# Attention on 64x64 array tiles in two shared PSUM banks, windows at a pitch of 64, no value masks, new order of all engines: a windowed-attention image kernel on one Trainium2 core

## What is computed

```python
def _swin_block(x, shift, mask, ...):
    sc = x
    x = _ln(x, ln1g, ln1b)
    if shift: x = jnp.roll(x, (-shift, -shift), axis=(1, 2))
    qkv = _win_part(x) @ qkvw + qkvb
    q, k, v = heads of 32 ...
    attn = jnp.einsum('whid,whjd->whij', q, k) * HEAD_DIM ** (-0.5)
    attn = softmax(attn + bias + mask)
    out = jnp.einsum('whij,whjd->whid', attn, v) ... @ projw + projb
    x = sc + roll_back(_win_rev(out))
    h = _ln(x, ln2g, ln2b)
    return x + gelu(h @ w1 + b1) @ w2 + b2
```

## Time and profile before

| | |
|---|---|
| median of 3 runs | 3472.59 us |
| lowest, highest | 3461.66, 10726.62 us |
| the profiled execution | 3461.46 us, of which its span is 3459.9 us |
| mean granted TensorE clock | 0.980 of 2.4 GHz |
| TensorE busy (matrix rows) | 3252.6 us, 94% of the span |
| TensorE weight loads | 2917.9 us, 84% |
| VectorE, ScalarE, GpSimd busy | 2319.8 (67%), 1835.4 (53%), 835.7 us (24%) |

### The profile page before, as it was taken

The page is one execution under the profiler, slowest core; times in us unless marked ns, Lnnn a source line. Parts: engine busy times, 40 slices in busy tenths (PEclk is TensorE's granted clock), DMA queues, the critical chain, the costliest instruction groups (busy, mean ns, idle before and its releaser), DMA issues. The chain is left out here.

```text
span 3459.9 us, 93945 instructions
## 1 busy us (share of the span) xinstructions
PE 3252.6 (94%) x35410; PEld 2917.9 (84%) x35410; DVE 2319.8 (67%) x6973; ACT 1835.4 (53%) x4329; POOL 835.7 (24%) x1402
## 2 busy tenths in 40 slices
PE   7996999999999999999999999999999999999689
PEld 6884788888888888888888888888888888888589
DVE  1114777777777777777777777777777777777332
ACT  1112566666666666666665555556555565555221
POOL 5301222222222222222222222222222222222010
PEclk9997999999999999999999999999999999999889
DMA  5321111111111111111211111111111111111275
GB/s 103 94 74 46 26 36 35 35 35 34 30 32 32 35 35 35 35 35 35 52 34 37 30 29 35 35 35 33 32 35 24 35 35 35 35 30 30 47 140 93
DMA packets 246673, 148.29 MB, mean 43 GB/s; under 512 B 31729, under 2 KB 246068, under 8 KB 246586
## 3 DMA queue, kind: packets, MB, share of 16 engines
q1 hardware_dynamic: 244882, 146.95, 18.9%
q0 software_dynamic: 1728, 0.48, 0.1%
HBM read 96.74 MB, written 52.50 MB: 43 GB/s over the span
## 5 line engine op out<-in xcount | busy, mean ns | idle before, releaser
L1427 PE MATMUL rm<-w,ht 128*112 128x160 f32 x4480 | 693.7, 304 | 0.0
L1427 PEld LDWEIGHTS rm<-w,ht 128*112 128x112 f32 x4480 | 608.8, 177 | 28.3 <-ACT ht L1010 12.7
L916 POOL TENSOR_TENSOR rs<-ln_tmp,mhalf 112x4 f32<-112x4 f32 (+1 forms) x128 | 125.5, 980 | 1728.1 <-DVE ln_tmp L1080 1728.1
L1010 ACT ACTIVATE ht<-rm 128x448 f32<-128x448 f32 (+1 forms) x640 | 318.7, 498 | 186.2 <-PE rm L111 180.1
L992 ACT ACTIVATE ot_hi<-ra 128x98 fp32r<-128x98 f32 x512 | 103.1, 258 | 456.2 <-PE ra L1406 456.2
L955 ACT ACTIVATE qm<-ra,qmask 128x392 f32<-128x392 f32 x512 | 258.6, 588 | 12.4 <-PE ra L111 3.3
L111 PE MATMUL rm<-z2t_hi,w_hi 128*128 128x448 f32 (+1 forms) x640 | 251.2, 393 | 2.6 <-DVE z2t_rest L1185 1.1
L1375 PE MATMUL s_ps<-kt,qm 128*49 128x49 f32 x8192 | 241.1, 211 | 0.9 <-DVE sc L1140 0.9
L1375 PEld LDWEIGHTS s_ps<-kt,qm 128*49 128x49 f32 x8192 | 209.1, 126 | 36.3 <-issue 30.9
L111 PE MATMUL rm<-z2t_rest,w_rest 98*128 98x448 f32 (+1 forms) x640 | 220.0, 344 | 0.0
L111 PE MATMUL rm<-z2t_hi,w_lo 128*128 128x448 f32 (+1 forms) x640 | 219.1, 342 | 0.0
(11 more groups left out here) (243 smaller groups left out, 9384.0 us busy)
## 6 DMA issues: line engine op xcount, KB each, us to landing
xa<-xs SPq DMA_DIRECT2D x128, 245.0 KB
xr<-xs SPq DMA_DIRECT2D x128, 245.0 KB
xs<-a_tok SPq DMA_DIRECT2D x8, 1960.0 KB, 9.5
xs<-xo SPq DMA_DIRECT2D x64, 245.0 KB
ys<-yz SPq DMA_DIRECT2D x64, 245.0 KB
c_y<-ys SPq DMA_DIRECT2D x48, 260.0 KB
c_y<-ys SPq DMA_DIRECT2D x16, 280.0 KB
c_taps<-in_f_syn SPq DMA_DIRECT2D x24, 126.0 KB, 5.2
```

The costliest lines, as they stand in the source:

```text
L916: gp.tensor_tensor(rs[1][:, t0:t0 + nt], ln_tmp[1][5][:, t0:t0 + nt], mhalf[:, 0:nt], ALU.pow).then_inc(s_pow, 1)
L1010: act_(ht[:, f * SN + t0 * TT:f * SN + (t0 + nt) * TT], bank_m(i, lm, use)[:, 0:nt * TT], ACT.Gelu_apprx_tanh).then_inc(m_freed(i, lm, use ...
L1427: last = mm(bank_m(i, lm, use)[0:TT, t * DIM:(t + 1) * DIM], ht[:, c:c + TT], keep.w["w2", lm][:, f * DIM:(f + 1) * DIM], start=(f == 0), ...
```

## The change

- Scores: the contraction runs over 64 partitions (two heads per half of the array, kept apart by a mask of two kinds, so two masked copies of the queries, not four); the fifth head lies twice, for the two rows of the array. The 20 products go in the order row half, column half, so four in a row lie in the four 64x64 quarters. Row half 0 writes one PSUM bank and row half 1 another.
- Outputs: contraction over 49 tokens of one window; p chooses the row half, w the column half: 20 products of 49x33 (40 rows), where 10 of 49x66 stood. They share the two banks with the scores (`so`), columns 256 and up, so scores and outputs of neighbouring groups wait for each other's readers (`s_sadd`, `s_od`).
- Tokens of a window pair lie at a pitch of 64. `values` has 128 stationary columns instead of 98; its masks go, and ScalarE alone evicts it, once. Queries and keys have 400 moving columns instead of 392.
- `weights_out` is one copy, the transposes use a permutation (`gather`), `pr` has two buffers; `fifth_head` is 4 copies of 196 columns, not 2 of 392.
- A `nop` stands behind the waits of scores and outputs on TensorE.
- The strips are loaded and stored in two blocks of 7 rows instead of even and odd rows; z1t, vb and pr are set once at the start of phase_b.
- The order of all three engines' lists is new. TensorE's: mlp_in, scores 2, mlp_out 0, front_turned 0, weights_turned 0, mlp_out 1, outputs 0, front_turned 1, weights_turned 1, mlp_out 2, outputs_turned 0, scores 3, mlp_out 3, outputs 1, weights_turned 2, Q0, outputs_turned 1, K0, outputs 2, weights_turned 3, mlp_out 4, outputs_turned 2, B0, outputs 3, mlp_out 5, outputs_turned 3, [linear 0, 1], projection 0, 1, Q1, projection 2, [linear 2, 3], and from K1 as before.

```diff
-        RA = Ring(["OT0", "OT1", "T1A0", "T1C0", "T1A1", "T1C1", "OT2", "Q0", "K0", "OT3", "P0", "P1", "B0", "Q1", "P2",
-                   "K1", "B1", "V0", "V1", "V2", "V3"], 3, V_READERS)
+        PRO = Ring(FRONT, 3, {})
+        RA = Ring(["T1A0", "T1C0", "T1A1", "T1C1", "OT0", "Q0", "OT1", "K0", "OT2", "B0", "OT3", "P0", "P1", "Q1", "P2",
+                   "K1", "B1", "V0", "V1", "V2", "V3"], 3, {})
         END = Ring(["OT0", "OT1", "OT2", "OT3", "P0", "P1", "P2"], 3, {})
...
-        QH = SN // 2
+        QH = QN // 2
...
                     act.wait_ge(*a_full(i, use))
-                    for h in range(4):
-                        last = act_(qm[:, h * SN + hf * QH:h * SN + (hf + 1) * QH], bank_a(i, use)[:, 0:QH], ACT.Copy,
-                                    scale=keep.qmask[:, h:h + 1])
+                    for odd in range(2):
+                        last = act_(qm[:, odd * QN + hf * QH:odd * QN + (hf + 1) * QH], bank_a(i, use)[:, 0:QH], ACT.Copy,
+                                    scale=keep.qpair[:, odd:odd + 1])
...
-                    cols = slice(hf * QH, (hf + 1) * QH)
-                    act_(q4[0:HD, cols], bank_a(i, use)[0:HD, 0:QH], ACT.Copy, scale=float(HD) ** -0.5)
-                    act_(k4[0:HD, cols], bank_a(i, use)[HD:2 * HD, 0:QH], ACT.Copy).then_inc(a_freed(i, use)[0], 1)
-
-                def values(j, p):
+                    dims = [[2 * WQ, 4], [1, WT]]
+                    for p in range(2):
+                        act_(view(q4, p * WP, HD, hf * QH + p * WQ, dims), view(bank_a(i, use), 0, HD, p * WQ, dims), ACT.Copy,
+                             scale=float(HD) ** -0.5)
+                        last = act_(view(k4, p * WP, HD, hf * QH + p * WQ, dims), view(bank_a(i, use), HD, HD, p * WQ, dims),
+                                    ACT.Copy)
+                    last.then_inc(a_freed(i, use)[0], 1)
...
-                    act_(pt[:, 0:4 * QP], pt_ps[0:GK, 0:4 * QP], ACT.Copy)
-                    act_(pt[:, 4 * QP:5 * QP], o_ps[0:GK, PT4:PT4 + QP], ACT.Copy).then_inc(s_pte, 1)
+                    act_(pt[:], pt_ps[0:QP, 0:HEADS * GK], ACT.Copy).then_inc(s_pte, 1)
...
                 if la is not None:
                     exps(0)
+                    exps(1)
+                if ln is not None:
+                    front_hi(0)
+                if la is not None:
                     weights_out(0)
-                    exps(1)
+                    exps(2)
+                if ln is not None:
+                    front_hi(1)
+                if la is not None:
+                    weights_out(1)
                     outputs_hi(0)
-                    weights_out(1)
-                    exps(2)
+                    weights_out(2)
+                    exps(3)
+                if ln is not None:
+                    queries(0)
+                if la is not None:
                     outputs_hi(1)
-                    weights_out(2)
-                if ln is not None:
-                    front_hi(0)
-                if la is not None:
-                    exps(3)
-                if ln is not None:
-                    front_hi(1)
-                if la is not None:
+                if ln is not None:
+                    keys(0)
+                if la is not None:
+                    weights_out(3)
                     outputs_hi(2)
-                    weights_out(3)
-                if ln is not None:
-                    queries(0)
-                    keys(0)
+                if ln is not None:
+                    fifth_head(0)
                 if la is not None:
                     outputs_hi(3)
                 if ln is not None:
-                    fifth_head(0)
                     queries(1)
-                if ln is not None:
                     keys(1)
                     fifth_head(1)
-                    values(0, 0)
-                if ln is not None:
-                    values(1, 0)
-                    values(2, 0)
+                    for j in range(3):
+                        values(j)
                 if la is not None:
                     t_hi(0)
                 if ln is not None:
-                    values(3, 0)
+                    values(3)
                 if la is not None:
                     t_hi(1)
...
+            for t, rows in zip(z1t, (128, 128, CR)):
+                v.memset(t[0:rows, :].bitcast(F32), 0.0)
+            v.memset(vb[:], 1.0)
+            for t in pr:
+                v.memset(t[:], 0.0)
...
-                    v.tensor_tensor(sc[:], s_ps[0:QP, 0:HEADS * GK], tab, ALU.add).then_inc(s_sadd, 1)
+                    v.tensor_tensor(view(sc, 0, QP, 0, [[SX, 2], [1, SX]]), view(so, 0, QP, 0, [[512, 2], [1, SX]]), tab,
+                                    ALU.add).then_inc(s_sadd, 1)
...
-                if lm is not None:
-                    mlp_out(0)
-                if la is not None:
-                    outputs(0)
+                if la is not None:
                     scores_biased(2, i, la)
                     scores_less_max(2, i)
                 if lm is not None:
+                    mlp_out(0)
+                if ln is not None:
+                    front_lo(0)
+                if lm is not None:
                     mlp_out(1)
                 if la is not None:
-                    outputs_lo(0)
-                    outputs(1)
-                    scores_biased(3, i, la)
-                    scores_less_max(3, i)
+                    outputs(0)
+                if ln is not None:
+                    front_lo(1)
                 if lm is not None:
                     mlp_out(2)
                 if la is not None:
-                    outputs_lo(1)
-                if ln is not None:
-                    front_lo(0)
-                if la is not None:
-                    outputs(2)
-                if ln is not None:
-                    front_lo(1)
+                    scores_biased(3, i, la)
+                    outputs_lo(0)
                 if lm is not None:
                     mlp_out(3)
                 if la is not None:
+                    outputs(1)
+                    scores_less_max(3, i)
+                    outputs_lo(1)
+                if lm is not None:
+                    mlp_out(4)
+                if la is not None:
+                    outputs(2)
                     outputs_lo(2)
                     outputs(3)
                 if lm is not None:
-                    mlp_out(4)
+                    mlp_out(5)
                 if la is not None:
                     outputs_lo(3)
-                if lm is not None:
-                    mlp_out(5)
...
                 if ln is not None:
-                    values(0, 1)
                     scores_biased(0, i + 1, ln)
-                    values(1, 1)
-                    values(2, 1)
                 if la is not None:
                     t_lo(0)
-                if ln is not None:
-                    values(3, 1)
-                if la is not None:
                     t_lo(1)
...
-                    filled_a(use, split_passes(nc, bank_a(i, use)[0:n, 0:QH], *[t[:, hf * QH:(hf + 1) * QH] for t in z1t],
+                    filled_a(use, split_passes(nc, bank_a(i, use)[0:n, 0:QH], *[view(t, 0, t.shape[0], hf * 4 * WP, [[8 * WP, 2], [WP, 4], [1, WQ]])
+                                                 for t in z1t],
...
-                        c = slice((2 * j + w) * GK, (2 * j + w + 1) * GK)
-                        last = split_passes(nc, bank_a(i, use)[0:GK, w * DIM:(w + 1) * DIM], *[t[:, c] for t in z1t], *wv, False)
+                        c = slice((8 * w + 2 * j) * WP, (8 * w + 2 * j + 2) * WP)
+                        last = split_passes(nc, bank_a(i, use)[:, w * DIM:(w + 1) * DIM], *[t[:, c] for t in z1t], *wv, False)
...
                     reach(pe, s_sadd, n * NG + j)
-                    for h in range(HEADS):
-                        for p in range(2):
+                    reach(pe, s_od, n * NG + {0: 0, 1: 0, 2: 0, 3: 1}[j])
+                    pe.nop(nofuse=True)
+                    for b in range(HEADS):
+                        for row in range(2):
+                            c0 = row * SX + b * WT
+                            h, p = SLOT.index(c0 // GK), c0 // WT % 2
+                            rows = slice(row * WP, (row + 1) * WP)
                             for w in range(2):
-                                c = (2 * j + w) * GK + p * WT
-                                q = qm[:, h * SN + c:h * SN + c + WT] if h < 4 else q4[:, c:c + WT]
-                                k = (kt if h < 4 else k4)[:, c:c + WT]
-                                last = mm(s_ps[w * WP:w * WP + WT, (2 * h + p) * WT:(2 * h + p + 1) * WT], q, k,
+                                c = j // 2 * QH + w * (4 * WQ) + (2 * (j % 2) + p) * WQ
+                                q = qm[rows, h % 2 * QN + c:h % 2 * QN + c + WT] if h < 4 else q4[rows, c:c + WT]
+                                k = (kt if h < 4 else k4)[rows, c:c + WT]
```

(19 more changed lines are left out.)

165 lines of the change are left out of this document (81 added, 84 removed).

## The result

The changed kernel takes 3520.15 us (median of 4 executions, 3517.03 to 3524.06) against 3467.54 us before: a ratio of 1.0158, 95% interval 1.0132 to 1.0184. The profiled execution took 3518.5 us, 57 us more than that of before; its mean granted clock is 0.969 (before 0.980). The forecast was 3545.

What follows compares the result with a forecast made beforehand. TensorE's list was taken to set the step; +1.6 us in 32 first-block steps and +0.9 in 32 second-block steps make 80 us, plus 4 once: 3461.5 + 84 = 3545 us. Forecast's own range 3490 to 3610; overall 3375 to 3700.

Steps and rivals of the forecast that it cites:

- middle case: Whole kernel: time about the same as before, between the bounds 3392 and 3531 us; chance 0.30.
- falls of the clock: Rival: TensorE's clock drops to 1.2 GHz after a third of 96 new gaps, 54 us, 3600 us; chance 10%.
- scores, four quarters: Scores pieces: 40 rows in 0.46 us, -0.46 us each, counted three times as scores 1 is hidden: -1.4 us a step.
- edges and nops: Small-tile runs on TensorE: 0.4 us a run, two more runs +0.65 us a step; eight nops +0.4.
- values, and mlp_turned 1's wait: Longer weight loads in 32 values products, +0.8 us a step; VectorE loses values evictions, -0.25 at mlp_turned 1.
- queries, keys, fifth head without the wait: Queries, keys and fifth head on TensorE stream 8 columns more in 24 products: +0.1 us a step.
- wait for qm: TensorE's wait before B1 for masked copies of the queries goes, two copies instead of four: -0.75 us, first block.
- small waits at front_turned: Two small TensorE waits, around outputs 2 and for ring room at front_turned 1, go: -0.5 us a step.
- outputs_turned 2 waits for os: Behind mlp_out 4, TensorE waits for VectorE's outputs(2), which stands behind outputs_lo(1) and mlp_out(4): +1.7 us a step.
- projection 0 waits for ot_rest: Without mlp_out 5 ahead of projection 0, TensorE waits for the splits: +1.45 us in the first block, 0 in the second.
- quarters do not run side by side: Rival: scores stay at 0.92 us and outputs go to 0.92, +2.8 us a step, 3722 us; chance 15%.
- edges vanish: Rival: costs at both ends of small-tile runs go, 7 runs x 0.4 = 2.8 us a step, 3366 us; chance 27%.

Runs made afterwards that it cites:

- e4: Changed kernel with scores 1, just ahead of mlp_in, issuing its products by array row, so two quarters at a time: 3523.7 us, ratio 1.0176.
- e3: Changed kernel with scores 2 issuing its products by array row, so two quarters at a time: 3550.3 us, ratio 1.0249.
- e2: Changed kernel with VectorE's outputs(2) moved ahead of outputs_lo(1) and mlp_out(4), nothing else: 3410.7 us, ratio 0.9845.
- e1: Changed kernel with mlp_out 5 put back behind outputs_turned 3, and outputs_lo(3) ahead of mlp_out(5) on VectorE: 3592.2 us, ratio 1.0368.
- e5: Changed kernel with five nops in place of one behind TensorE's waits ahead of scores and outputs: 3521.4 us, ratio 1.0162.
- e6: Changed kernel with 113 stationary columns in place of 128 in the products of values: 3524.6 us, ratio 1.0178.
- e9: Changed kernel with 14 transposes nobody reads behind outputs_turned 3 in the first block: 3505.8 us, ratio 1.0114.
- e7: Changed kernel reordered on three engines to cover both new waits, with the divisions of outputs 2 and 3 earlier on VectorE: 3355.3 us, ratio 0.9681.
- e8: e7 with 113 stationary columns in place of 128 in values: 3347.5 us, ratio 0.9656.
- e11: e9 with 12 more unread transposes between mlp_out 4 and outputs_turned 2 in both blocks: 3491.9 us, ratio 1.0090.
- e10: e8 with scores 0 of the next strip moved behind mlp_turned 0, and scores_biased(0) behind t_lo(1) on VectorE: 3529.9 us, ratio 1.0198.

## Why the prediction came out as it did

3545 us forecast, 3520 measured: 0.7% off and inside the forecast's own range. Slower by 1.6% is just inside the middle case (the bound was 3531), which had 30%, where slower by over 2% had 50%. But that the sum is so near is luck: the edges, put 1.05 us a step too high, are 67 us in 64 steps, and the queries' pieces and the falls of the clock, 0.47 us a step and 28 us that the sum did not have, are 58 us the other way.

The table sets the measured pieces of the first block, as medians over the steps without a fall, against the terms of the prediction. Scores and outputs are taken from the first start of their rows to the last, and what lies around them is put under edges.

| term | forecast, us | measured, us |
|---|---|---|
| scores, four quarters | -1.4 | -1.3 |
| outputs | -0.5 | -0.45 |
| edges and nops | +1.05 | about 0 |
| values, and mlp_turned 1's wait | +0.8 - 0.25 | +0.37 |
| queries, keys, fifth head without the wait | +0.1 | +0.57 |
| wait for qm | -0.75 | -0.75 |
| small waits at front_turned | -0.5 | -0.6 |
| outputs_turned 2 waits for os | +1.7 | +1.6 |
| projection 0 waits for ot_rest | +1.45 | +1.3 |
| sum | +1.7 (taken: 1.6) | +0.7 |
| falls of the clock | 0 (rival, 10%) | +0.78 |
| step | 46.2 | 46.03 |

- *Four quarters.* Right: 40 rows from the first start to the last in 0.470 us, 12 ns a row, where 0.46 was said; and scores 1 is hidden (e4). The rival "quarters do not run side by side" is refuted by the rows, and e3 prices it at 0.31 us for a piece, by an estimate from it about 1 us a step in all. The Trainium skill (TensorE: Matmul & The Clock Gate, "Wait — 56ns, not 53.3ns?") puts the floor of start to start near 25 ns; these rows average 12 ns, so as a limit on all starts the rule doesn't hold here. The trace has the rows four at a time, one group every 46 ns or so; before and in e3, with two quarters at work, it is a pair every 46 ns. A limit of one row in 46 ns for each quarter fits all three. A floor of 23.5 ns for a product of two rows would fit the four quarters as well and would not bind with two; no run excludes it.
- *Both new waits.* Right in place, releaser and size, 1.6 for 1.7 and 1.9 us idle for 1.8, and for the reason given: e2 takes the first away by moving `outputs(2)` in VectorE's list, and nothing else; e1 brings the second from 1.8 us down to 0.46 by putting mlp_out 5 back over it.
- *Edges and nops* is the step that failed, +1.05 for about nothing. A piece of small tiles costs 0.135 us more than its rows (0.605 less 0.470), not 0.4; the transposes of weights that stood ahead of scores or outputs got 0.2 us shorter in all; what mlp_out pays beside small tiles (0.09 to 0.18 a piece, 0.1 more in all than before) and the scores that used to run straight into outputs (0.1) take it back, and nops cost nothing (e5). The price of a nop was an estimate from the length of a wait, which no row shows either. The Trainium skill (TensorEngine Tiling (Array Packing), "Key Properties") says that a change of tiling mode drains the engine; the trace agrees in kind, with 0.1 to 0.2 us at each piece. So the rival "edges vanish" did not come true: the edges are still there at 0.1 to 0.2 us, and 7 pieces at 0.4 were never there to be saved. What failed is the price of a run and of a nop, and it shows most in the second block, where the step was to be 47.3 us and is 46.42 without a fall.
- *Queries* is the term that was too small: cutting Q0, K0 and B0, Q1 apart with other pieces between them costs 0.15 and 0.27 us, for restarts and for the 8 columns (no run tells these two apart); K1 and B1 have 0.1 more.
- *Values.* The spacing went from 87 to 113-116 ns, +0.8 us by the rows as said, and 0.2 of it lies under the wait of mlp_turned 1.
- *The clock.* A rival of 10% turned out to be half the result. Its price was put well (1.7 us a fall; 1.55 measured), its frequency too high: about a third of 96 gaps were to be followed by a fall, and 19 were (18 in the two stretches and one between them), so 28 us and not 54. The reason against it, that phase_b has 2 us of transposes without a fall, was no argument about idle time. In the profiles of the changed kernel, e6 and e9 each fall of the first block begins 1 to 2 us behind the end of one of the two gaps; none stands elsewhere. What picks the gaps that are followed by one is not shown: the same gap of 1.43 us ahead of outputs_turned 2 is followed by 16 falls in 31 steps of the first block of e9, and by 1 in 27 of its second.
- *Second block.* +0.9 was said; steps without a fall are as long as before (46.42), since +1.05 for edges was too much there as well. From first mlp_in to last the second block takes 8 us more than before, by its few falls, the first block 45 us, and the first mlp_in of all starts 4.6 us later (the +4 of the memsets): the 57 us between the profiled executions.

The rows of scores and outputs save 1.8 us a step, by an estimate from the table some 115 us or 3% of the kernel. No run has the new tiles in the old order, so what tiles and masks give by themselves is not shown. The new order gives the saving back at two places where TensorE waits for VectorE; with these mended it is 3.2% faster than before (e7), and 3.4% with narrower values too (e8).

## What to carry to other kernels

When pieces are moved on the bounding engine, write down for each wait what the releasing engine does in the microsecond before; an in-order list with the wanted instruction third in line is a wait of the two ahead of it (e2: one line, 110 us). A gap on TensorE of 1.5 us is not priced by its length alone: the clock may fall behind it (28 us in e11), and a saving of a few tenths elsewhere can go under in falls (e6). Before pricing such a saving, look at what the next piece waits for: in the first block of e6 it was GpSimd. Take a cover away only after asking what else it covers (e1), and in a shared bank, who has to read before the next write (e10).
